# A four-layer network of graph convolutions and experts on one core: result rows of the experts stored by token from GpSimd, and record copies moved to ScalarE

## The reference, cut to what matters

```python
# layer 0, edges: a filter for every edge, a gather, a product, a segment sum
h = x @ W_in2f
Wij = (ssp(rbf @ Wf1 + bf1) @ Wf2 + bf2) * dist_cut
m = segment_sum(h[idx_j] * Wij, idx_i)
# layers 0 and 1, experts: the best two of 8 for every token
for e in range(8):
    out = out + w[:, e:e+1] * (gelu(xf @ W1[e] + b1[e]) @ W2[e] + b2[e])
# layer 3, experts: the best one of 8, and only while pos < C (C = 1.25 * T / 8)
buf = zeros(E, C, D).at[idx, pos].set(x, mode='drop')
y_tok = (relu(buf @ w1 + b1) @ w2 + b2)[idx, min(pos, C - 1)] * (prb * kept)
x = x + y
```

## Time and profile before

| | |
|---|---|
| median of 3 runs | 6599.27 us (6598.04 to 6601.91) |
| the profiled execution | 6604.11 us, its span 6602.2 us |
| busy in the span | PE 75%, DVE 65%, POOL 46%, ACT 41% |
| edges of layer 0 | about 671 to 1508 us, 110 batches |
| groups of layer 0 | about 1760 to 2020 us, 32 groups |
| groups of layer 1, then its combining | about 3631 to 4291 us, 32 groups; to 4366 us |
| groups of layer 3, then its combining | about 6278 to 6519 us, 16 groups; to 6587 us |

### The profile page before, as it was taken

The page is one execution under the profiler, slowest core; times in us unless marked ns, Lnnn a source line. Parts: engine busy times, 40 slices in busy tenths (PEclk is TensorE's granted clock), DMA queues, the critical chain, the costliest instruction groups (busy, mean ns, idle before and its releaser), DMA issues. The chain is left out here.

```text
span 6602.2 us, 121404 instructions
## 1 busy us (share of the span) xinstructions
PE 4976.5 (75%) x25835; PEld 3743.8 (57%) x25900; DVE 4291.8 (65%) x13483; ACT 2699.2 (41%) x7737; POOL 3069.5 (46%) x3707
## 2 busy tenths in 40 slices
PE   5730899994574478888883899949989997888594
PEld 4520676673443356666662666625656775666484
DVE  7771788884685679999996777743432114888613
ACT  0010677773114336666662111114523332788421
POOL 2777777776474048888870111043210000777212
PEclk7565999997696689999995999969988998999697
DMA  9221444455586222222232555533410001666363
GB/s 340 54 66 42 118 120 120 121 118 102 124 242 159 64 57 69 68 68 69 68 60 74 171 188 189 170 105 114 136 56 15 14 10 47 160 161 160 74 188 110
DMA packets 845518, 724.26 MB, mean 110 GB/s; under 512 B 404456, under 2 KB 750962, under 8 KB 844962
## 3 DMA queue, kind: packets, MB, share of 16 engines
q1 hardware_dynamic: 589612, 364.61, 19.7%
q0 software_dynamic: 119056, 282.67, 16.1%
q10 hardware_dynamic: 136678, 75.06, 3.8%
HBM read 520.38 MB, written 201.60 MB: 109 GB/s over the span
## 5 line engine op out<-in xcount | busy, mean ns | idle before, releaser
L992 POOL DMA_INDIRECT l3e_rows<-table,l3e_idx x440 | 434.1, 987 | 788.7 <-DVE l3e_idx L1014 660.4
L992 POOL DMA_INDIRECT l0e_rows<-table,l0e_idx x440 | 436.9, 993 | 121.0 <-issue 99.4
L992 POOL DMA_INDIRECT l1e_rows<-table,l1e_idx x440 | 429.6, 976 | 121.3 <-issue 121.3
L3247 ACT ACTIVATE l1e_weighted<-l1e_rows,l1e_power 128x64 f32<-128x64 f32 x1760 | 463.0, 334 | 16.6 <-ACT l1e_power L3238 11.6
L765 POOL DMA_INDIRECT records_by_src<-l0n_rec_src,l0n_pos_at_src x390 | 397.8, 1020 | 115.4 <-issue 108.8
L1270 PE MATMUL l0e_ps_w<-l0e_wf,l0e_hidT 128*128 128x256 f32 x1760 | 410.6, 387 | 0.3 <-PE l0e_ps_s L1281 0.3
L1270 PEld LDWEIGHTS l0e_ps_w<-l0e_wf,l0e_hidT 128*128 128x128 f32 x1760 | 326.8, 191 | 123.7 <-issue 84.0
L2075 DVE SCALAR_TENSOR_TENSOR net_x<-l2fe_ps_y,l2f_mix,net_x 128x256 f32 x200 | 96.7, 484 | 425.5 <-PE l2fe_ps_y L2002 364.7
L3188 PE MATMUL l1e_ps_row<-net_ident,l1e_logit 128*128 128x128 f32 x1760 | 277.1, 281 | 127.5 <-DVE l1e_logit L3383 126.0
L2038 ACT ACTIVATE l2fe_hT<-l2fe_ps_h,l2fe_own,l2fe_own 128x320 f32<-128x320 f32 x320 | 197.4, 617 | 314.4 <-PE l2fe_ps_h L1990 314.4
L2625 ACT ACTIVATE l1fg_hT<-l1fg_ps_h,l1fg_b_cols 128x256 f32<-128x256 f32 x256 | 107.3, 470 | 526.3 <-PE l1fg_ps_h L2568 526.3
(11 more groups left out here) (811 smaller groups left out, 14912.0 us busy)
## 6 DMA issues: line engine op xcount, KB each, us to landing
counts<-l1f_total ACTq DMA_DIRECT2D x272, 128.0 KB, 4.5
l1fg_w_in<-in_L_ffn_W SPq DMA_DIRECT2D x32, 1024.0 KB
l1fg_w_out<-in_L_ffn_W SPq DMA_DIRECT2D x32, 1024.0 KB, 5.6
records_by_dst<-l0n_blank_dst SPq DMA_DIRECT2D x1, 32560.0 KB, 93.3
l3e_rec<-records_by_dst SPq DMA_DIRECT2D x110, 296.0 KB, 3.4
l2d_counts<-counts SPq DMA_DIRECT2D x208, 128.0 KB, 2.5
l2d_counts<-counts POOLq DMA_DIRECT2D x192, 128.0 KB, 2.8
l3fg_w_in<-in_L_ffn_w SPq DMA_DIRECT2D x16, 1024.0 KB, 5.2
```

The lines of the kernel that those rows point to most:

```text
L992: pool.indirect_dma_start(at(self.rows[b], k, self.width), None, self.table, bass.IndirectOffsetOnAxis(self.idx[b][:, k:k + 1], 0)).then_i ...
L3247: act.activation(out[:, h, 0:each], g.rows[b][:, lo:lo + each], ACT.Copy, scale=power[b][:, m * heads + h:m * heads + h + 1])
```

## The change

Four edits are made.

1. Layer 0, edges: `Scatter.copy` of GpSimd becomes `copy_by_scalar` on ACT, first in each ACT iteration (lag 0). GpSimd runs the gathers of batch t and then the scatter of batch t-1. PE no longer waits for its own sums; DVE's `hot` waits for `summed` instead.
2. Layer 0, groups: the same copy goes to ACT, at lag 0, ahead of `activate`.
3. Layers 1 and 3, groups: result rows are stored by token and choice. `TokenOfSlot` also works out `target_of`, the row of `outputs` for each slot (out of bounds for an empty slot). GpSimd stores `y` with two indirect transfers per group (`put_by_four`, lag 2); ACT's plain store is gone. DVE waits for `aimed` in place of `stored`. The indirect stores have a bounds check.
4. Layers 1 and 3, combining: since `outputs` is now in token order, SP (and ACT for the second choice) load it with plain transfers, five blocks of tokens each. In layer 3 the second set of slots (`slot_out`) is no longer computed.

```diff
+    def copy_by_scalar(self, act, q, i, b):
+        to = self.to
+        act.wait_ge(self.loaded[b], (i + 1) * 16 * len(to.fields))
+        act.sem_inc(self.tick, 1)
+        act.activation(tiled(self.rec[b][:, :], to.width)[:, :, to.number:to.width],
+                       to.meta[:, self.taken(i, b, META)].rearrange("p (j r) -> p j r", r=META), ACT.Copy).then_inc(self.copied, 1)
+        act.activation(self.pos_at[b][:, :], to.pos[:, self.taken(i, b, 1)], ACT.Copy).then_inc(self.copied, 1)
...
@@ l0_gnn_edges
-            with pool.Fori(0, NB // RING) as i:
-                for b in range(RING):
-                    scatter.copy(pool, i * RING + b, i, b)
-                    g.gather_batch(pool, i * RING + b, b)
-                    scatter.scatter(pool, i * RING + b, b)
+            skewed(pool, (0, lambda q, i, b: g.gather_batch(pool, q, b)), (1, lambda q, i, b: scatter.scatter(pool, q, b)))
...
+            def hot(q, i, b):
+                if not isinstance(i, int) or i:
+                    dve.wait_ge(summed, (q - RING) * TWO + TWO)
+                mark_nodes(dve, net, g.onehot[b], g.column(b, g.placed.near)).then_inc(g.hot_ready, 1)
...
-                pe.wait_ge(summed, q * TWO + TWO)
-                pe.sem_inc(g.hot_free, 1)
...
-            skewed(act, (1, power), (0, turn), (4, flush))
+            skewed(act, (0, lambda q, i, b: scatter.copy_by_scalar(act, q, i, b)), (1, power), (0, turn), (4, flush))
@@ choose, capacity
-                    link(dve.tensor_scalar(ahead[:, :], ahead[:, :], float(CAPACITY - 1), None, ALU.min))
-                    link(dve.tensor_tensor(rest[:, :], ahead[:, :], two[:, :], ALU.add))
-                    place(one, rest, to.slot_out[0][:, :])
@@ TokenOfSlot.keep
+        if self.to.by_token:
+            link(dve.tensor_scalar(self.over[:, :], self.token[:, :], float(P), float(4 * NP), ALU.is_lt, ALU.mult))
+            link(dve.scalar_tensor_tensor(self.over[:, :], self.token[:, :], -float(P), self.over[:, :], ALU.add, ALU.add))
+            link(dve.tensor_copy(self.to.target_of[:, :], self.over[:, :]))
+            link(dve.tensor_scalar(self.token[:, :], self.token[:, :], -float(P), 0.0, ALU.add, ALU.max))
+            link(dve.tensor_scalar(self.over[:, :], self.token[:, :], float(NP), -float(NP), ALU.is_ge, ALU.mult))
+            link(dve.tensor_tensor(self.token[:, :], self.token[:, :], self.over[:, :], ALU.add))
@@ moe_groups
+                if not to.by_token:
+                    act.wait_ge(y_ready, (g + 2) * TILES)
+                    act.dma_start(to.outputs[bass.ds(g * SLICE, SLICE), :].rearrange("(t p) d -> p t d", p=P),
+                                  tiled(y[b][:, :], D)).then_inc(stored[b], 16)
+            skewed(act, (0, copy), (0, activate), (1, store), (2, store_rows), **run)
...
-                dve.wait_ge(stored[b], (i + 1) * 16)
+                if to.by_token:
+                    dve.wait_ge(aimed, g + 1)
+                else:
+                    dve.wait_ge(stored[b], (i + 1) * 16)
...
+            def put_by_four(g, i, b):
+
+                if not isinstance(g, int) or g >= 2:
+                    pool.wait_ge(stored[b % 2], (i * 2 + b // 2) * ROWS)
+                pool.sem_inc(pool_tick, 1)
+                pool.tensor_copy(target[b % 2][:, :], at(to.target_of, g, TILES)).then_inc(aimed, 1)
+                pool.wait_ge(aimed, g + 1)
+                pool.wait_ge(y_ready, (g + 2) * TILES)
+                pool.sem_inc(pool_tick, 1)
+                for t in range(TILES):
+                    pool.indirect_dma_start(to.outputs, bass.IndirectOffsetOnAxis(target[b % 2][:, t:t + 1], 0),
+                                            at(y[b % 2], t, D), None, bounds_check=to.choices * NP - 1,
+                                            oob_is_err=False).then_inc(stored[b % 2], 16)
...
-            skewed(pool, (1, copy), (0, pick), (1, scatter_out), **run)
+            if to.by_token:
+                skewed(pool, (0, pick_by_four), (2, put_by_four), ring=4, total=to.groups)
+                for b in range(2):
+                    pool.wait_ge(stored[b], to.groups // 2 * ROWS)
+            else:
+                skewed(pool, (0, pick), (1, scatter_out), **run)
@@ moe_combine
-            for t in range(NT):
-                for c in range(to.choices):
-                    pool.indirect_dma_start(at(rows[c], t, D), None, to.outputs,
-                                            bass.IndirectOffsetOnAxis(to.slot_out[c][:, t:t + 1], 0)).then_inc(gathered[t // UN], 16)
+        def bring(eng, c):
+            for i in range(NI):
+                whole = UN if i < NI - 1 else UN - 1
+                eng.dma_start(tiled(at(rows[c], i, UN * D)[:, 0:whole * D], D),
+                              node_rows(to.outputs, c * NT + i * UN, whole)).then_inc(brought[i], 16)
+            eng.wait_ge(blank, to.choices)
+            eng.dma_start(at(rows[c], NT - 1, D)[0:TAIL, :],
+                          to.outputs[c * NP + (NT - 1) * P:c * NP + N, :]).then_inc(brought[NI - 1], 16)
```

More of the change, by code:

```diff
@@ L2299, with __init__ @@
 class Dispatch:
-    def __init__(self, net, s, choices, groups, capacity, xn):
+    def __init__(self, net, s, choices, groups, capacity, xn, by_token):
         self.choices, self.groups, self.capacity, self.xn = choices, groups, capacity, xn
         self.slot_in = [s.sb(f"slot_in{c}", [P, NT], I32) for c in range(choices)]
-        self.slot_out = [s.sb(f"slot_out{c}", [P, NT], I32) for c in range(choices)] if capacity else self.slot_in
         self.weight = [s.sb(f"weight{c}", [P, NT]) for c in range(choices)]
@@ L2309, in __init__ @@
         self.tokens = net.dispatch["tokens"][0:NP, :]
-        self.outputs = net.dispatch["outputs"][0:groups * SLICE, :]
+        self.by_token = by_token
+        self.target_of = s.sb("target_of", [P, groups * SLICE // P], I32) if by_token else None
+        self.outputs = net.dispatch["outputs"][0:choices * NP if by_token else groups * SLICE, :]
 class TokenOfSlot:
@@ L2324, in __init__ @@
         self.place = s.sb("pull_place", both)
-        self.id_i = s.sb("pull_id_i", [P, NT + 1], I32)
-        self.id = s.sb("pull_id", [P, NT + 1])
+        self.blocks = to.choices * NT if to.by_token else NT
+        self.id_i = s.sb("pull_id_i", [P, self.blocks + 1], I32)
+        self.id = s.sb("pull_id", [P, self.blocks + 1])
+        self.over = s.sb("pull_over", [P, self.rows])
         self.token = s.sb("pull_token", [P, self.rows])
@@ L2500, in moe_groups @@
         now = [s.sb(f"now{b}", [P, TILES], I32) for b in range(2)]
+        target = [s.sb(f"target{b}", [P, TILES], I32) for b in range(2)]
+        aimed = s.sem("aimed")
         ROWS = 16 * TILES
@@ L2608, in _ @@
             act.sem_inc(active, HALVES)
-            for b in range(2):
+            for b in range(0 if to.by_token else 2):
                 act.sem_inc(stored[b], 16)
@@ L2634, in store_rows, with copy @@
             def store_rows(g, i, b):
-                act.wait_ge(y_ready, (g + 2) * TILES)
-                act.dma_start(to.outputs[bass.ds(g * SLICE, SLICE), :].rearrange("(t p) d -> p t d", p=P),
-                              tiled(y[b][:, :], D)).then_inc(stored[b], 16)
-            skewed(act, (0, activate), (1, store), (2, store_rows), **run)
+                if not to.by_token:
+                    act.wait_ge(y_ready, (g + 2) * TILES)
+                    act.dma_start(to.outputs[bass.ds(g * SLICE, SLICE), :].rearrange("(t p) d -> p t d", p=P),
+                                  tiled(y[b][:, :], D)).then_inc(stored[b], 16)
+            def copy(g, i, b):
+                if beside:
+                    scatter.copy_by_scalar(act, g, i, b)
+            skewed(act, (0, copy), (0, activate), (1, store), (2, store_rows), **run)
             if counting:
                 counting.end_scalar(act)
-            for b in range(2):
+            for b in range(0 if to.by_token else 2):
                 act.wait_ge(stored[b], 16 * (to.groups // 2 + 1))
@@ L2703, in _ @@
         def _(pool):
-            def copy(g, i, b):
-                if beside:
-                    scatter.copy(pool, g, i, b)
             def scatter_out(g, i, b):
```

40 lines of the change are left out of this document (26 added, 14 removed).

## The result

| | before | after |
|---|---|---|
| median | 6600.59 us (6598.04 to 6610.45, 4 runs) | 6646.74 us (6643.96 to 6648.07, 4 runs) |
| ratio | | 1.0065, 95% interval 1.005 to 1.0081 |
| span of the profiled execution | 6602.2 us | 6644.2 us |

The 42.0 us between the two profiled spans can be laid out by stage, from the first and last starts of the same instructions in both traces. A positive number is time lost.

What follows compares the result with a forecast made beforehand. PE and POOL were taken to run without slack in layer 0's edges, at 7.5 us a batch. Terms -25 - 7 + 30 + 8 - 39 - 3 + 1 = -35 us brought 6599.3 to 6564 us; range 6534 to 6590.

Steps and rivals of the forecast that it cites:

- 13 x 2.3 = 30 us: Groups of layer 3: PE waits 2.3 us for late rows in each of groups 3 to 15, 30 us lost.
- here I take 3.2: Groups of layer 3: gathered rows land 3.2 us after the second gather, so they are there at 8.4 us.
- landing 5.6: Groups of layer 3, upper bound: landing takes 5.6 us, giving a wait of 4.7 us a group and 61 us lost.
- 3 us of cover: Groups of layer 1: rows come at 8.4 us, PE wants them only at 11.56, so 3.2 us cover the chain.
- Edges of layer 0: Edges of layer 0: POOL becomes the bound at about 7.3 us a batch, gaining 25 us; ACT's copies just fit.
- Groups of layer 0: Groups of layer 0: without the copies the pick's own copy starts 0.26 us earlier in 32 groups; 7 us gained.
- layer 1: Groups of layer 1: indirect transfers running while DVE marks lengthen the marks; 8 us lost.
- its combining: Combining of layer 1: plain loads replace 50 gathers, 70.9 us become 32; 39 us gained.
- combining of layer 3: Combining of layer 3: DVE's wait for its first rows falls from 8.75 to 6.0 us; 3 us gained.
- chain of layer 3: Groups of layer 3, from `y`: stores at 0.75 and 2.02 us, end 2.97, gathers at 3.94 and 5.21, rows at 8.4.
- The rival that layer 3 loses more: Groups of layer 3: landing of 5.6 us costs 31 us more, kernel at 6595 us; chance 9%.
- DVE's marks stop layer 1: Groups of layer 1: marks stretch POOL's transfers, rows 2.1 us late in 29 groups, 61 us, kernel at 6625; chance 7%.

Runs made afterwards that it cites:

- w_in_late: The changed kernel, with layer 3's w_in load issued only when PE has turned the rows of the group before: 6613.7 us, ratio 1.0025 to the kernel before.
- spread_rows: The changed kernel, with each empty slot picking the token row of its partition's number instead of row 0: 6596.3 us, ratio 0.9993 to the kernel before.
- pick_first: The changed kernel, with GpSimd in layers 1 and 3 storing rows of group t-3, not t-2, after pick t: 6550.1 us, ratio 0.9928 to before.
- spare_rows: pick_first, with each empty slot of layer 3 storing to its own spare row behind the results: 7439.3 us, 7468.1 for the kernel before beside it.
- spread_late: The changed kernel, with spread_rows and w_in_late together: 7471.1 us, 7468.1 for the kernel before beside it.

## Why the prediction was wrong

**The step that failed** is "13 x 2.3 = 30 us", in two places. Its landing, "here I take 3.2", came from the median of another stage, 3.7, and leaned down; the full groups of layer 3 do land in 3.0 us, and the other eleven of the thirteen in 3.8 to 6.5 us. With 5.58 us to the second gather and 6.54 for its landing in the group shown PE starts at 12.12 us after `y`, where it could have at 6.45: 5.67 and not 2.3. The bound of "landing 5.6" gave 4.7 us and 61 us and was nearly the wait that was measured, 58.0, but partly by luck: it took the weight load for the cause and knew nothing of the shared row. And I let it have 9 in 100. What I needed was in the kernel, not in a row: which addresses the index list holds, and that SP issues w_in just then. I had named w_out.

The second place was in no bound at all. A stall was priced as its own length, but in 12 of the 13 groups PE, which had stopped at 1.00, resumed at 0.50. The price here is 1.5 times the wait, 88 for 58; with the shorter waits of w_in_late and spread_rows it is 1.4 times (55.0 for 40.5, 37.7 for 26.9).

**Order and mechanism** were right: rows late in layer 3 in 13 groups, released by `l3fg_rows`, none in layer 1 (3 us of cover held), and pick_first shows that nothing else was lost in layer 3.

**Edges of layer 0.** POOL became the bound, as said, at 4 x (1.024 + 0.30) + 1.6 x (1.034 + 0.30) = 7.43 us a batch and not 7.3: the gathers had been taken at their old 993 ns. That eats 0.13 x 110 = 14 of the 25 us. ACT's copies were hidden. That the two parts need each other I didn't see, nor that the gathers are shorter with PE's wait (993 and 987 ns in the mean) than without it (1037 and 1024). What stretches them isn't shown.

**The rest.** Groups of layer 0 8 (7 predicted), layer 1 5 (8), its combining 38 (39). In the combining of layer 3 the way from `y` to the loads was taken as the stores' landing alone; the stage doesn't end before GpSimd's drain behind them has, 5.3 us, which makes it a loss of 3. The same term stood in the combining of layer 1, where the drain takes 1.7 us. In the chain of layer 3 the second store's end is 2.02 + 0.97 = 2.99 us, not 2.97; that changes nothing.

**The rival that layer 3 loses more** was the right one, at 6595 too cheap by the clock and by layer 0. That DVE's marks stop layer 1 didn't come: its gathers rose from 972 to 1172 ns in the median, 0.2 us each, inside the cover. Its argument against itself, that the marks leave no room for stretched transfers, didn't hold in layer 1.

## What to carry to other kernels

When work is put in front of a prefetch on an in-order engine, add a stage of lag for it in the same edit: here one number, 2 to 3, was worth 97 us, and made a loss of 46 into a gain of 49. Price a stall of PE above its length, by the clock behind it. And look at what padding reads: with indices that nearly all name one row the gathers landed in 3.9 to 4.3 us, and in 5.7 to 6.5 with the w_in load right behind them, where distinct rows took 2.8 to 3.3. A full stage of cover hid all of it.

## What the runs showed of the hardware

- 192 packets of GpSimd's queue took 59 us of engine time where most of the gathered rows were one and the same row and a weight load ran beside; 32 us with the load later; 15 us with distinct rows.
- Taking away a wait of PE made GpSimd's gathers longer (993 to 1037 ns) and the kernel slower by 17 us.
- Extra products of zeros in the stalls (5.2 us a group) made the stage shorter, by 19 us from the first `l3fg_y` on. After waits of 2.0 to 2.4 us PE resumed at the lower clock in 5 of 13 groups, after waits of 2.1 to 5.7 us in 12 of 13.
- GpSimd's drain at the end of a block: with indirect stores 1.7 us in layer 1 and 5.3 in layer 3, the same in each run; without them 5.3 in layer 1 (one run) and 2.7 in layer 3.
- The kernel before took 6596 to 6601 us on some chips and 7405 to 7468 on others. The groups of layer 3 are equally long on both to 0.1 us (pick_first and spare_rows 209.4, spread_rows and spread_late 247.1 and 247.0); pick_first's order gained 0.7% on the one, spare_rows, which has it too, 0.3% on the other.
